# State-space mixer with expert feed-forward: scores as fp32r products over stacked halves, and zero-padded carried states

## The chip, the cores and the metric

The kernel runs on one core of one Trainium2 chip, as one launch. The metric is the device time of that launch in microseconds. The core has five engines with instruction streams of their own: PE (TensorE, matrix products), DVE (VectorE), ACT (ScalarE), POOL (GpSimd) and SP, which here only issues DMAs. They meet through semaphores.

## The reference, cut to what matters

16 sequences (called batches below) of 512 tokens with 128 channels pass through a state-space mixer, a layer norm, a routed mixture of 12 experts and a second layer norm. Everything is float32.

```python
ssm_in = x @ Win                     # gives B_ssm, C_ssm (64 each), dt_raw (8 heads), X (8 heads x 64)
delta = softplus(dt_raw + dt_bias)
# per time step and head:
h = exp(delta * neg_A) * h + X_t * (delta * B_t)
y_t = einsum('bhpn,bn->bhp', h, C_t)
y = y + D_param * X
output = (y * (silu(x @ Wz) @ Wzg)) @ Wout
x = layernorm(x + output)
# experts: hidden = gelu(sum_e dw1[:, e] * x @ W1[e].T); y = sum_e dw2[:, e] * hidden @ W2[e].T
x = layernorm(x + y + dw3 @ b2)
```

## The kernel before, in words

A batch's 512 tokens are cut into four chunks of 128. The scan becomes products: within a chunk, scores `G = B C^T` (four products of 128 x 128, `mix_scores`, L756) are weighed by decays per head and multiplied with `X` (`mix_y_within`, L920); between chunks, a state of 64 numbers per head channel is carried (`mix_states`, L802) and multiplied with the decayed `C` (`mix_y_carried`, L924). Most products are kept exact by splitting an operand into a rounded half `hi` and the rest `lo`, and running three fp32r products (`mm3`, L253 to L255); scores, both y products and the output projection are plain fp32, and each such product shows as two records in the trace.

The order of work on every engine is written out by hand in `body` (L1383). One call of it interleaves the experts of batch p with the mixer of the next batch b. Its order around the change: the last outputs of the experts of the batch before p; scores, decay rates (`mix_rates`) and chunk ends (`mix_ends`) of b; then expert 0 of p (`expert_in`, four banks of 3 products), the gate `mix_zg`, experts 1 and so on up to 11, with the heads of b between them. For each expert e, one preparation runs ahead of the products (`expert_prep`): SP fetches a row of routing weights by DMA (L1190), DVE multiplies (L1207, sends `xw`), ACT rounds (L1237, `xw_hi`), POOL takes the rest (L1241, `xw_lo`), and PE waits for `xw_lo`. For each head h, ACT scales the scores (L843), DVE adds the skip term (L852) and scans the decays (L870), POOL multiplies the two (L881, `W`). Engines take their instructions strictly in this order, so whatever stands ahead on DVE delays the next expert's multiply.

`mix_rates` also forms a running product on DVE (L710) that SP sends out and fetches back as rows (L724, L728, L747, L753); the row for expert 3 stands behind these on SP. Two PSUM banks (`mix_bank`) serve the mixer's products in turn, in the order of the table `MIX_USES`; each use waits for the reader of the one before in its bank. In the first call of `body` (b = 1) scores and rates were done ahead. Of the 16 batches, 14 (b = 2 to 15) run scores inside `body`, and 15 (b = 1 to 15) the carried products.

Of the kernel before, what the change touches and what calls it, by code (L numbers as in the profile page):

```python
# [15 lines left out]
P = 128  # L16
D = 128
NB, T = 16, 512
NC = T // P
# [23 lines left out]
    + [("X3", "Xd", 4), ("st01", "state", 2), ("st2", "state", 3)]  # L43
# [42 lines left out]
def layer_program(nc, x, Wz, Win, Wzg, Wout, dt_bias, A_log, D_param, P_w, U1T, U2T, U3T, W1T, W2T, b2, out):  # L86
    ctx = ExitStack()
    with ctx:
# [91 lines left out]
        for name, n in dict(  # L180
# [4 lines left out]
            ps_st=2, state=NC - 1, st_tmp=NC - 2, ctd=NQ, scan=H, G_dt=H, W=H,  # L185
# [8 lines left out]
        product("G_skip", H, 1, 1)  # L194
        product("xw", E, less=2)
# [62 lines left out]
        def mix_number(i, use):  # L258

            n = MIX_USE[use] % NX  # L260
            return NX - 1 - n if i == 0 and use in ("BC", "dtB") else n
# [347 lines left out]
        def mix_bc(eng, b):  # L609
# [83 lines left out]
        def mix_rates(eng, b, start=True):  # L693
# [10 lines left out]
            if eng is DVE:  # L704
# [63 lines left out]

        def mix_ends(eng, b):
# [32 lines left out]
        def mix_states(eng, b):  # L802
# [15 lines left out]
            if eng is DVE:  # L818
                for c, (use, at, k) in enumerate(place):
                    ps = bank_of(use, b)[:, at:at + N]  # L820
                    wait(DVE, "ps_st", b, k)
                    wait(DVE, "ps_ys", b.prev())
                    if c == 0:
                        sig("state", DVE.tensor_copy(S[:, 0, :], ps))
                    else:
                        wait(DVE, "state", b, c)
                        sig("st_tmp", DVE.tensor_tensor(
                            St[:, :].rearrange("p (q n) -> p q n", n=HD), S[:, c - 1, :].rearrange("p (q n) -> p q n", n=HD),
                            total[:, c * NQ:(c + 1) * NQ].unsqueeze(2).to_broadcast([P, NQ, HD]), ALU.mult))
# [1050 lines left out]
```

How the kernel before makes its waits and increments, by code:

```python
        def wait(eng, name, b, k=None):  # L219
            p = prods[name]
            v = (b.off - p.start) * p.n * p.step + ((p.n if k is None else k) - p.less) * p.step
            seen = waited.setdefault(id(eng), {})
            if (b.reg is None and v <= 0) or seen.get(name, -10**9) >= v:
                return
            seen[name] = v
            eng.wait_ge(p.sem, v if b.reg is None else b.reg * (p.n * p.step) + v)
            if eng is SP:
                alone(SP)
# [75 lines left out]
        def round_rest(n, src, hi, lo):  # L305
            DVE.tensor_copy(hi, src).then_inc(sems["chain"], 1)
            DVE.wait_ge(sems["chain"], n)
            DVE.tensor_tensor(lo, src, hi.bitcast(F32), ALU.subtract).then_inc(sems["cast"], 1)
# [1 line left out]
        def setup(eng):  # L311
# [3 lines left out]
                SP.dma_start(st_wz, Wz[:, :]).then_inc(sems["wz"], 16)  # L315
                SP.dma_start(bias_b[:, :], dt_bias.partition_broadcast(P)).then_inc(sems["decay_par"], 16)
                SP.dma_start(neg_a[:, :], A_log.partition_broadcast(P)).then_inc(sems["decay_par"], 16)
                SP.dma_start(d_b[:, :], D_param.partition_broadcast(P)).then_inc(sems["decay_par"], 16)
                SP.dma_start(st_wzg, Wzg.rearrange("(k p) n -> p k n", p=P)).then_inc(sems["wzg"], 16)
                SP.wait_ge(sems["pad"], 5)
                SP.dma_start(dA_dram.rearrange("h (c t) -> (h c) t", t=P), cum_t[0:H * NC, :]).then_inc(sems["zero"], 16)
                SP.dma_start(pw, P_w[:, :]).then_inc(sems["small"], 16)
```

## Time and profile before

| what | value |
|---|---|
| median of 3 runs | 1521.87 us (1521.78 to 1521.9) |
| the profiled execution, its own time | 1522.09 us |
| its span, first to last instruction | 1520.4 us |
| PE busy | 1504.6 us, 99% |
| DVE busy | 1128.1 us, 74% |
| POOL, ACT busy | 655.8 us, 43%; 606.0 us, 40% |
| mean granted TensorE clock | 0.999 |

"Busy" counts matrix products from start to modelled end, and these overlap, so PE at 99% says that it hardly ever stood empty. All stretches below lie in one ordinary batch between 619 and 712 us.

### The profile page before, as it was taken

To read this page: it belongs to the slowest core of one execution; us is meant where nothing else is said; L and a number is where in the kernel's file an instruction comes from. 1 tells how busy PE (TensorE), PEld (TensorE's weight loads), DVE (VectorE), ACT (ScalarE), POOL (GpSimd) and SP (SyncE) were. 2 spreads that over 40 slices of the span, in tenths; PEclk is the share of its full clock that TensorE was granted. 3 is DMA by queue.
4 is the path that set the end of the run, shared out by engine and by line. 5 is a ranking of instruction groups with operands and counts; after the bars stand their busy time and mean duration, and the time that the engine had idled before them with its cause. 6 is when DMAs were issued, how large, how long until landed. Compare 5 with 4: busy or idle time off the path is not lost.

```text
span 1520.4 us, 25377 instructions
## 1 busy us (share of the span) xinstructions
PE 1504.6 (99%) x8630; PEld 1250.7 (82%) x8630; DVE 1128.1 (74%) x3186; ACT 606.0 (40%) x1376; POOL 655.8 (43%) x747
## 2 busy tenths in 40 slices
PE   8999999999999999999999999999999999999998
PEld 7778888888888878888888888888888888888876
DVE  7797676967768677686876769777686776868755
ACT  6752424425244351533525244252443515335130
POOL 6771634616245270643606346162451715436040
PEclk9999999999999999999999999999999999999999
DMA  5350312314023040321404123140231403214020
GB/s 170 109 162 22 121 41 68 102 29 138 17 80 92 28 139 15 105 72 46 122 14 125 45 65 105 29 131 24 74 95 30 139 15 99 77 42 125 18 77 7
DMA packets 81505, 114.55 MB, mean 75 GB/s; under 512 B 10168, under 2 KB 37344, under 8 KB 81376
## 3 DMA queue, kind: packets, MB, share of 16 engines
q1 hardware_dynamic: 81376, 112.93, 24.6%
q8 instruction: 68, 1.11, 0.3%
q14 instruction: 61, 0.50, 0.1%
HBM read 107.77 MB, written 5.13 MB: 74 GB/s over the span
## 4 chain that ended last, share of the span: by engine, by line
PE 93%; POOL 2%; DVE 2%; DMA 1%; issue 1%; ACT 0%; SPq 0%; POOLq 0%; DVEq 0%; ACTq 0%
PE exp_bank L253 23%; PE exp_bank L255 22%; PE exp_bank L254 22%; PE mix_bank L964 4%; PE mix_bank L920 4%; PE mix_bank L253 3%; PE mix_bank L255 3%; PE mix_bank L254 3%; PE mix_bank L933 3%; PE mix_bank L814 1%; PE mix_bank L545 1%; PE mix_bank L762 1%; PE mix_bank L1056 1%; PE mix_bank L524 0%; POOL Wt L881 0%
## 5 line engine op out<-in xcount | busy, mean ns | idle before, releaser
L1241 POOL TENSOR_TENSOR sp_lo<-fbuf,sp_hi 128x512 fp32r<-128x512 f32 (+2 forms) x201 | 243.2, 1214 | 169.5 <-ACT sp_hi L1237 104.2
L253 PE MATMUL exp_bank<-w_hi,sp_hi 128*128 128x512 f32 x768 | 303.9, 396 | 1.2 <-POOL sp_lo L1294 0.8
L253 PE MATMUL exp_bank<-sp_hi,w_hi 128*128 128x512 f32 x764 | 302.8, 396 | 0.8 <-POOL sp_lo L1241 0.7
L255 PE MATMUL exp_bank<-w_hi,sp_lo 128*128 128x512 f32 x768 | 299.8, 390 | 0.0
L254 PE MATMUL exp_bank<-w_lo,sp_hi 128*128 128x512 f32 x768 | 299.0, 389 | 0.0
L255 PE MATMUL exp_bank<-sp_hi,w_lo 128*128 128x512 f32 x764 | 297.8, 390 | 0.0
L254 PE MATMUL exp_bank<-sp_lo,w_hi 128*128 128x512 f32 x764 | 297.5, 389 | 0.0
L1345 DVE SCALAR_TENSOR_TENSOR acc<-exp_bank,dw,acc 128x128 f32<-128x128 f32 x384 | 132.4, 345 | 163.6 <-PE exp_bank L255 162.8
L1237 ACT CAST sp_hi<-fbuf 128x512 fp32r<-128x512 f32 (+2 forms) x203 | 120.0, 592 | 270.7 <-DVE fbuf L1207 214.5
L881 POOL TENSOR_TENSOR Wt<-Wt,Gh 128x512 f32<-128x512 f32 x128 | 185.3, 1449 | 29.9 <-DVE Wt L870 29.9
L579 POOL TENSOR_TENSOR delta<-delta,bias_b 128x32 f32<-128x32 f32 x16 | 4.0, 253 | 414.3 <-ACT delta L555 409.2
L253 PEld LDWEIGHTS exp_bank<-sp_hi,w_hi 128*128 128x128 f32 x764 | 143.4, 188 | 39.3 <-issue 8.8
L870 DVE TENSOR_TENSOR_SCAN Wt<-seg_b,unit_bank 128x512 f32<-128x512 f32 x125 | 150.7, 1207 | 32.4 <-PE mix_bank L920 29.2
L255 PEld LDWEIGHTS exp_bank<-w_hi,sp_lo 128*128 128x128 f32 x768 | 144.1, 188 | 31.0
L253 PEld LDWEIGHTS exp_bank<-w_hi,sp_hi 128*128 128x128 f32 x768 | 144.3, 188 | 30.6 <-POOL sp_lo L1294 1.3
L843 ACT ACTIVATE Gh<-Gm,delta 128x128 f32<-128x128 f32 x512 | 163.7, 391 | 13.2 <-POOL Wt L881 13.2
L255 PEld LDWEIGHTS exp_bank<-sp_hi,w_lo 128*128 128x128 f32 x764 | 143.4, 188 | 30.6
L254 PEld LDWEIGHTS exp_bank<-w_lo,sp_hi 128*128 128x128 f32 x768 | 144.4, 188 | 29.0
L254 PEld LDWEIGHTS exp_bank<-sp_lo,w_hi 128*128 128x128 f32 x764 | 143.5, 188 | 28.5
L1207 DVE TENSOR_TENSOR fbuf<-turn_bank,row_b 128x512 f32<-128x512 f32 x189 | 127.1, 674 | 14.7 <-DMA row_b<-dw_rows 14.0
L1345 DVE SCALAR_TENSOR_TENSOR acc_odd<-exp_bank,dw,acc_odd 128x128 f32<-128x128 f32 x320 | 109.2, 341 | 0.0
L852 DVE SCALAR_TENSOR_TENSOR Gh<-unit_bank,d_b,Gh 128x512 f32<-128x512 f32 x120 | 88.4, 736 | 0.9 <-ACT Gh L843 0.8
(276 smaller groups left out, 2228.1 us busy)
## 6 DMA issues: line engine op xcount, KB each, us to landing
row_b<-dw_rows SPq DMA_DIRECT2D x189, 256.0 KB, 3.3
seg_b<-dA_rows SPq DMA_DIRECT2D x125, 256.0 KB, 3.4
ctd<-cum_rows SPq DMA_DIRECT2D x128, 96.0 KB, 3.2
x_in<-in_x SPq DMA_DIRECT2D x16, 256.0 KB, 2.7
result<-acc SPq DMA_DIRECT2D x15, 256.0 KB, 2.2
fbuf<-in_W1T SPq DMA_DIRECT2D x12, 256.0 KB, 4.0
acc<-in_W2T SPq DMA_DIRECT2D x4, 256.0 KB, 3.5
x_in<-in_W2T SPq DMA_DIRECT2D x4, 256.0 KB, 2.8
```

The costliest lines, as they stand in the source:

```text
L253: nc.tensor.matmul(ps, s_hi, m_hi, start=start and j == 0, stop=False, skip_group_check=onto)
L254: nc.tensor.matmul(ps, s_hi, m_lo, start=False, stop=False, skip_group_check=onto)
L255: last = nc.tensor.matmul(ps, s_lo, m_hi, start=False, stop=stop and j == n - 1, skip_group_check=onto)
L843: last = AC.activation(G[:, c, :], Gm[:, c, :], ACT.Copy, scale=delta[:, c, h:h + 1])
L852: sig("G_skip", DVE.scalar_tensor_tensor(flat, unit[:, :], d_b[:, h:h + 1], flat, ALU.mult, ALU.add))
L870: sig("scan", DVE.tensor_tensor_scan(W, first_seg[h] if first(b) else seg_b[h % 2][:, :], unit[:, :], 0.0, ALU.mult, ALU.add))
L881: sig("W", PO.tensor_tensor(W, W, Gh[h % 2][:, :, :].rearrange("p c t -> p (c t)"), ALU.mult))
L920: last = PE.matmul(ps[j * HD:(j + 1) * HD, tok(c)], Xd[:, c, h * HD:(h + 1) * HD], Wt[:, q % 2, at:at + P], start=False, stop=not opens an ...
L1207: sig("xw", DVE.tensor_tensor(wide[e % 2], rb[:, :], row_b[e % 2][:, :], ALU.mult))
L1237: sig("xw_hi", AC.copy(hi[:, cols], wide[e % 2][:, cols]))
L1241: sig("xw_lo", on.tensor_tensor(lo[:, cols], wide[e % 2][:, cols], hi[:, cols].bitcast(F32), ALU.subtract))
L1345: sig("comb", DVE.scalar_tensor_tensor(dst, ps, w, dst, ALU.mult, ALU.add))
```

## The change

Scores, from batch 2 on. ACT writes the rounded `B` to partitions 0 to 63 of a tile `BS` and DVE its rest to partitions 64 to 127; ACT and POOL write `C` rounded and rest side by side into `CS`. One fp32r product per chunk, 128 rows deep and 256 columns wide, gives two partial scores side by side, and DVE adds them with a reduction (two instructions, in place of ACT's copy `Gm`). The four products are issued in two halves: two behind rates and ends, two inside expert 0, behind its third bank. The running product moves behind both reductions on DVE. `BS` and `CS` lie in the memory of `zg`.

Carried states, from batch 1 on. Each head half has a tile of its own of 128 rows, zero in the other half's rows, so that the carried products are 128 deep, as those within a chunk are. The tiles of the first two states (`S_wide`) lie in the memory of `xT_hi` and `xT_lo`; POOL sets them to zero in each batch, ahead of expert 4's split. ACT copies the first state (two instructions), behind the scaled scores of head 0; DVE computes the other two in a new function `mix_carry`, seven instructions, which stands behind the scan of head 0, where `mix_states` stood ahead of expert 4's multiply with five.

```diff
+        S_wide = nc.alloc_sbuf_tensor_at("S_wide", [P, 2, 2, NQ * HD], F32, offset=halves_at)
...
+                if later(b):
+                    wait(AC, "ps_out", b.prev())
+                    sig("B_hi", AC.copy(BS[0:NS, :], bank_of("BC", b)[0:NS, :]))
...
+                sig("B_lo", DVE.tensor_tensor(BS[NS:2 * NS, :], bank_of("BC", b)[0:NS, :], BS[0:NS, :].bitcast(F32), ALU.subtract))
...
+                sig("C_hi", AC.copy(CS[:, 0, :], CT[:, :]))
...
+                sig("C_lo", PO.tensor_tensor(CS[:, 1, :], CT[:, :], CS[:, 0, :].bitcast(F32), ALU.subtract))
...
+        def mix_scores_half(eng, b, n):
...
+                wait(PE, "B_lo", b)
+                wait(PE, "C_lo", b)
+                ps = mix_bank(b, use)
+                for j in range(2):
+                    at = tok(2 * n + j)
+                    last = PE.matmul(ps[:, 2 * j * P:2 * (j + 1) * P].rearrange("p (k t) -> p k t", k=2), BS[:, at], CS[:, :, at],
+                                     start=True, stop=True)
+                sig("ps_G2", last)
+            if eng is DVE:
+                wait(DVE, "ps_G2", b, n + 1)
+                wait(DVE, "G_dt", b.prev())
+                sig("Gm2", DVE.tensor_reduce(Gm[:, cs, :], bank_of(use, b)[:, :].rearrange("p (c k t) -> p c t k", c=2, k=2), AX.X, ALU.add))
...
+                sig("S_zero", PO.memset(S_wide[:, :, :, :], 0.0))
+            if eng is AC and not first(b):
+                wait(AC, "ps_st", b, 1)
+                wait(AC, "S_zero", b)
+                wait(AC, "ps_ys", b.prev())
+                for j in range(2):
+                    n = slice(j * NS, (j + 1) * NS)
+                    copied = AC.copy(S_pad[0][n, j, :], bank_of("st01", b)[n, 0:N])
+                sig("state_0", copied)
...
+        def mix_carry(eng, b):
...
+                sig("st_tmp", DVE.tensor_tensor(groups(St[:, :]), groups(ps0), total_of(1), ALU.mult))
+                wait(DVE, "st_tmp", b, 1)
+                for j, n in enumerate(rows_of):
+                    last = DVE.tensor_tensor(S_pad[1][n, j, :], St[n, :], ps1[n, :], ALU.add)
+                sig("state", last)
+                wait(DVE, "state", b, 1)
+                for j, n in enumerate(rows_of):
+                    last = DVE.tensor_tensor(groups(St[n, :]), groups(S_pad[1][n, j, :]), total_of(2, n), ALU.mult)
+                sig("st_tmp", last)
+                wait(DVE, "ps_st", b, 2)
+                wait(DVE, "st_tmp", b, 2)
+                for j, n in enumerate(rows_of):
+                    last = DVE.tensor_tensor(S_pad[2][n, j, :], St[n, :], bank_of("st2", b)[n, 0:N], ALU.add)
+                sig("state", last)
...
+                    n = slice(j * NS, (j + 1) * NS) if first(b) else slice(0, P)
+                    state = (S[n, c - 1] if first(b) else S_pad[c - 1][:, j])[:, q * HD:(q + 1) * HD]
...
-                mix_scores(eng, b)
                 mix_silu_split(eng, b)
                 mix_rates(eng, b)
                 mix_ends(eng, b)
+                mix_scores_half(eng, b, 0)
+                if eng is DVE:
+                    mix_scores_half(DVE, b, 1)
+                    mix_running_product(b)
...
-                expert_in(eng, p, 0)
+                expert_in(eng, p, 0, lambda hc: hc == 2 and mix_scores_half(PE, b, 1))
...
-            mix_states(eng, b)
             if norm_before or eng is not AC:
                 mix_score_step(eng, b, 0)
+            mix_states(eng, b)
...
             mix_decay(eng, b, 0)
+            mix_carry(eng, b)
```

PE, around expert 0, before. The first three rows end the experts of the batch before; L762 are the scores, L698 to L776 rates and ends, and the next rows expert 0 (`sp_hi`, `sp_lo` are its halves).

```order
L255 MATMUL exp_bank<-w_hi,sp_lo 128x512
L762 MATMUL mix_bank<-CT,BT 128x128 x4
L698 MATMUL mix_bank<-ident,a_rows 32x128
L775 MATMUL mix_bank<-a_parts,strict_r 128x64
L776 MATMUL mix_bank<-a_parts,one_r 128x64
L253 MATMUL exp_bank<-sp_hi,w_hi 128x512
```

The same place on PE now; line numbers are those of the changed kernel (L739, L839, L840 are rates and ends, L825 the scores, L268 to L270 the three products of a split pair).

```order
L270 MATMUL exp_bank<-w_hi,sp_lo 128x512
L739 MATMUL mix_bank<-ident,a_rows 32x128
L839 MATMUL mix_bank<-a_parts,strict_r 128x64
L840 MATMUL mix_bank<-a_parts,one_r 128x64
L825 MATMUL mix_bank<-CS,BS 128x256 x2
L268 MATMUL exp_bank<-sp_hi,w_hi 128x512
```

Two of the four score products left the place between the batches, and two more (L825 again) stand inside expert 0, ahead of its fourth bank.

DVE, from the multiplies of experts 2 and 3 to that of expert 5, before:

```order
L1207 TENSOR_TENSOR fbuf<-turn_bank,row_b 128x512 x2
L824 COPY S<-mix_bank 128x256
L827 TENSOR_TENSOR St<-S,total 128x256
L831 TENSOR_TENSOR S<-St,mix_bank 128x256
L827 TENSOR_TENSOR St<-S,total 128x256
L831 TENSOR_TENSOR S<-St,mix_bank 128x256
L1207 TENSOR_TENSOR fbuf<-turn_bank,row_b 128x512
L852 SCALAR_TENSOR_TENSOR Gh<-unit_bank,d_b,Gh 128x512
L870 SCALAR_TENSOR_TENSOR Wt<-seg_b,unit_bank 128x512
L888 TENSOR_TENSOR ctd<-ctd,CT 128x384
L1207 TENSOR_TENSOR fbuf<-turn_bank,row_b 128x512
```

The same stretch of DVE now: L1318 is the experts' multiply, L958 the skip term, L976 the scan, L924 to L936 the carry, L994 the decayed C.

```order
L1318 TENSOR_TENSOR fbuf<-turn_bank,row_b 128x512 x3
L958 SCALAR_TENSOR_TENSOR Gh<-unit_bank,d_b,Gh 128x512
L976 SCALAR_TENSOR_TENSOR Wt<-seg_b,unit_bank 128x512
L924 TENSOR_TENSOR St<-mix_bank,total 128x256
L927 TENSOR_TENSOR S_wide<-St,mix_bank 64x256 x2
L931 TENSOR_TENSOR St<-S_wide,total 64x256 x2
L936 TENSOR_TENSOR S<-St,mix_bank 64x256 x2
L994 TENSOR_TENSOR ctd<-ctd,CT 128x384
L1318 TENSOR_TENSOR fbuf<-turn_bank,row_b 128x512
```

The state work moved from ahead of expert 4's multiply to between the multiplies of experts 4 and 5, and grew from five instructions to seven.

POOL, from the chunk-end products to head 0's product, now (before, there was no MEMSET, and L1241 stood there four times):

```order
L862 TENSOR_TENSOR Wt<-Xd,ends 128x512 x3
L1352 TENSOR_TENSOR sp_lo<-fbuf,sp_hi 128x512 x3
L887 MEMSET S_wide 128x1024
L1352 TENSOR_TENSOR sp_lo<-fbuf,sp_hi 128x512
L987 TENSOR_TENSOR Wt<-Wt,Gh 128x512
```

The memset came in between the splits of experts 3 and 4.

## Rows read from the trace of the kernel before

**Rows 1.** The page, part 1: busy time, share of span, instructions.

```profile
PE 1504.6 (99%) x8630; PEld 1250.7 (82%) x8630; DVE 1128.1 (74%) x3186; ACT 606.0 (40%) x1376; POOL 655.8 (43%) x747
```

**Rows 2.** Waits of PE: who for whom, us in total, times, longest.

```profile
PE exp_bank L253 <- POOL sp_lo L1241: 0.7, 1, 0.7
```

**Rows 3.** Timeline of PE: start us, us, engine, line, operation, operands, count.

```profile
619.59 1.05 PE L762 MATMUL mix_bank<-CT,BT 128*128 128x128 f32 x8
...
620.73 0.48 PE L253 MATMUL exp_bank<-sp_hi,w_hi 128*128 128x512 f32 x1
621.05 0.39 PE L254 MATMUL exp_bank<-sp_lo,w_hi 128*128 128x512 f32 x1
...
622.89 0.39 PE L253 MATMUL exp_bank<-sp_hi,w_hi 128*128 128x512 f32 x1
...
642.94 0.39 PE L253 MATMUL exp_bank<-sp_hi,w_hi 128*128 128x512 f32 x1
...
665.56 0.40 PE L1303 MATMUL turn_bank<-b_tab,bias_rows 128*128 128x256 f32 x2
665.88 1.53 PE L933 MATMUL mix_bank<-ctd,S 64*64 64x128 f32 x24
667.34 1.97 PE L920 MATMUL mix_bank<-Wt,Xd 128*64 128x128 f32 x32
```

**Rows 4.** Timeline of ACT, same batch.

```profile
619.79 0.30 ACT L1237 CAST sp_hi<-fbuf 128x128 fp32r<-128x128 f32 x1 [3.78 <-PE exp_bank L255]
...
637.47 0.62 ACT L1237 CAST sp_hi<-fbuf 128x512 fp32r<-128x512 f32 x1 [2.87 <-DVE fbuf L1207]
```

**Rows 5.** Timeline of POOL, same batch.

```profile
620.16 0.46 POOL L1241 TENSOR_TENSOR sp_lo<-fbuf,sp_hi 128x128 fp32r<-128x128 f32 x1 [2.93 <-ACT sp_hi L1237]
...
638.17 1.28 POOL L1241 TENSOR_TENSOR sp_lo<-fbuf,sp_hi 128x512 fp32r<-128x512 f32 x1 [3.05 <-DVE Gh L852]
639.42 1.61 POOL L881 TENSOR_TENSOR Wt<-Wt,Gh 128x512 f32<-128x512 f32 x1
...
661.67 1.61 POOL L881 TENSOR_TENSOR Wt<-Wt,Gh 128x512 f32<-128x512 f32 x1
```

**Rows 6.** Timeline of DVE, same batch.

```profile
622.76 0.67 DVE L710 TENSOR_TENSOR_SCAN cum_t<-dA_t,one 32x128 f32<-32x128 f32 x1
...
632.07 0.69 DVE L1207 TENSOR_TENSOR fbuf<-turn_bank,row_b 128x512 f32<-128x512 f32 x1 [0.21 <-DMA row_b<-dw_rows]
...
635.95 0.42 DVE L827 TENSOR_TENSOR St<-S,total 128x256 f32<-128x256 f32 x1
636.41 0.42 DVE L831 TENSOR_TENSOR S<-St,mix_bank 128x256 f32<-128x256 f32 x1
636.75 0.68 DVE L1207 TENSOR_TENSOR fbuf<-turn_bank,row_b 128x512 f32<-128x512 f32 x1
637.35 0.74 DVE L852 SCALAR_TENSOR_TENSOR Gh<-unit_bank,d_b,Gh 128x512 f32<-128x512 f32 x1
638.01 1.21 DVE L870 TENSOR_TENSOR_SCAN Wt<-seg_b,unit_bank 128x512 f32<-128x512 f32 x1
639.14 0.73 DVE L888 TENSOR_TENSOR ctd<-ctd,CT 128x384 f32<-128x384 f32 x1
639.79 0.68 DVE L1207 TENSOR_TENSOR fbuf<-turn_bank,row_b 128x512 f32<-128x512 f32 x1
...
661.25 0.87 DVE L888 TENSOR_TENSOR ctd<-ctd,CT 128x384 f32<-128x384 f32 x1
662.04 1.25 DVE L1006 TENSOR_TENSOR nrm<-nrm 128x4 f32<-128x4 f32 x1
```

**Rows 7.** Timeline of SP's DMA issues: four rows merged, the first for expert 3.

```profile
628.41 9.42 SPq L1190 DMA_DIRECT2D row_b<-dw_rows  x4
```

**Rows 8.** The page, part 6: DMA issues, KB each, median us to landing.

```profile
row_b<-dw_rows SPq DMA_DIRECT2D x189, 256.0 KB, 3.3
```

**Rows 9.** Groups of POOL by line and form: busy us, mean ns.

```profile
L335 POOL MEMSET BT<- 128x512 f32 x1 | 0.5, 517 | 0.0
```

More of the change, by code:

```diff
@@ L47 @@
 MIX_USE = {u[0]: n for n, u in enumerate(MIX_USES)}
+MIX_LATER = (
+    MIX_USES[:MIX_USE["G"]] + [("rates", "ends", 1), ("G01", "Gm2", 1), ("G23", "Gm2", 2)] + MIX_USES[MIX_USE["X2"]:]
+)
+MIX_LATER[MIX_USE["BC"]] = ("BC", "B_lo", 1)
+LATER_USE = {u[0]: n for n, u in enumerate(MIX_LATER)}
 MIX_FIRST = (
-    MIX_USES[:MIX_USE["X2"] + 1] + [("X3", "Xd", 4), ("st01", "state", 2), ("st2", "state", 3)]
+    MIX_USES[:MIX_USE["X2"] + 1] + [("X3", "Xd", 4), ("st01", "state", 1), ("st2", "state", 2)]
     + MIX_USES[MIX_USE["st2"] + 1:]
@@ L194, in layer_program @@
         product("G_skip", H, 1, 1)
+        for name, n in dict(ps_G2=2, Gm2=2, B_hi=1, B_lo=1, C_hi=1, C_lo=1).items():
+            product(name, n, 1, 2)
+        product("S_zero", 1, 1, 1)
         product("xw", E, less=2)
@@ L289, in first, with later @@
             return b.reg is None and b.off == 0
+        def later(b):
+            return b.off >= 2
         def bank_of(use, b):
@@ L708, in mix_rates @@
                 sig("end_sum", DVE.tensor_reduce(a_sums[:, :, :, :].rearrange("p k c h -> p k (c h)"), parts, AX.X, ALU.add))
-                wait(DVE, "rates_out", b.prev())
-                sig("ecum", DVE.tensor_tensor_scan(cum_t[R1, :], dA_t[R1, :], one[R1, :].to_broadcast([H * NC, P]),
-                                                   1.0, ALU.mult, ALU.mult))
+                if not later(b):
+                    mix_running_product(b)
             if eng is SP:
@@ L717, in mix_rates, with mix_running_product @@
                     start_rows(eng, b)
+        def mix_running_product(b):
+            wait(DVE, "dA", b)
+            wait(DVE, "rates_out", b.prev())
+            sig("ecum", DVE.tensor_tensor_scan(cum_t[R1, :], dA_t[R1, :], one[R1, :].to_broadcast([H * NC, P]),
+                                               1.0, ALU.mult, ALU.mult))
         def rates_out(b, part):
@@ L821, in mix_states @@
                     wait(DVE, "ps_st", b, k)
-                    wait(DVE, "ps_ys", b.prev())
                     if c == 0:
-                        sig("state", DVE.tensor_copy(S[:, 0, :], ps))
-                    else:
[L826 to L829, printed above, removed]
+                        sig("state_0", DVE.tensor_copy(S[:, 0, :], ps))
@@ L830, in mix_states, with groups, total_of @@
+                        wait(DVE, "state_0", b)
+                    else:
+                        wait(DVE, "state", b, c - 1)
+                        sig("st_tmp", DVE.tensor_tensor(groups(St[:, :]), groups(S[:, c - 1, :]), total_of(c), ALU.mult))
                         wait(DVE, "st_tmp", b, c)
                         sig("state", DVE.tensor_tensor(S[:, c, :], St[:, :], ps, ALU.add))
+        def groups(v):
+            return v.rearrange("p (q n) -> p q n", n=HD)
+        def total_of(c, n=slice(0, P)):
+            return total[n, c * NQ:(c + 1) * NQ].unsqueeze(2).to_broadcast([n.stop - n.start, NQ, HD])
@@ L836, in mix_score_step @@
             if eng is AC:
-                wait(AC, "Gm", b)
+                wait(AC, "Gm2" if later(b) else "Gm", b)
                 if h >= 2:
@@ L1852, in layer_program @@
         for p in prods.values():
-            written = 1 if p.name.startswith("end") and p.start else 3 if p.name != "x_in" else 2
+            written = 1 if p.name.startswith("end") and p.start else 3 if p.name not in ("x_in", "ps_G", "Gm") else 2
             count = p.done + p.less
```

65 lines of the change are left out of this document (54 added, 11 removed).

## The prediction

> **What bounds the kernel now.** I read the page first: PE is busy for 99% of the span, DVE for 74% [rows 1]. Then the waits of PE: one wait of 0.7 us for an expert's rest half is among its longest in 1520 us [rows 2], so in an ordinary batch PE runs without a gap, and its own instructions are the time. Two things can move it: fewer or cheaper products, and a new wait. For the second I read one batch on all engines in order of time, and asked at each place that the change touches how much later PE's supplier may come.
>
> **Scores, on PE.** Four fp32 products take from 619.59 to about 620.48, when the rates begin: 0.89 us, 0.11 per record [rows 3]. The new ones are 256 columns of fp32r. The only such row is L1303: two in 0.40 us with the drain of the last (0.28), so 0.12 apart; up to the next group at 665.88 it is 0.16 each, with a change of tile shape in it [rows 3]. I take 0.11 to 0.12. Four cost 0.46 in place of 0.89: 0.43 us a batch, 6.0 us over 14 batches, if nothing else held PE.
>
> Something does. Expert 0 needs the rest of its last token chunk. Its source is read by PE's last product of the batch before, so ACT starts only behind that, at 619.79 for 0.30 [rows 4], and POOL follows at 620.16 for 0.46, to 620.62 [rows 5]. PE starts expert 0 at 620.73 [rows 3], about 0.1 us after POOL is done. So the 1.14 us of scores, rates and ends ahead of it just cover this chain, which the change leaves alone. With two score products of 0.23 in place of 0.89, PE has 0.48 us to do there and then waits some 0.66. Expert 0 still starts at 620.7, and the other two products now stand inside it as pure addition: 0.23, and 0.09 because a wide product behind short ones is followed late (620.73 to 621.05 is 0.32, where wide ones come 0.23 apart) [rows 3]. Scores therefore cost PE +0.31 a batch and gain nothing.
>
> **Carried products, on PE.** They keep their count, 24 records, and their columns. Solve two groups for pace and opening: L933 runs 1.53 us with 0.27 drain over 11 steps of two records, L920 1.97 over 15 [rows 3]; so a step is 0.11 in both, and the opening of each costs 0.05. Depth 64 or 128 makes no difference to the pace. Between the groups, L933's last step starts at 667.14 and L920 at 667.34: 0.09 more than a step. With one shape in both, opening and gap go: 0.14, twice a batch, 0.28 us, times 15 batches: -4.2 us. The bounds are 0 (the gap belongs to the wait for W) and 0.4 a batch.
>
> The Trainium skill, TensorEngine Tiling (Array Packing), Key Properties, says that a change of tiling mode drains the engine, and its table of speedups credits small contraction depth with up to 2x. By the first, the gain above is right; by the second, padding to 128 rows could double these products. The trace speaks for the first alone, since L920 at depth 128 keeps L933's pace; the second is the last rival below.
>
> **DVE, ACT, POOL, SP: first, how late the state becomes.** The other score product of expert 0 starts at 622.89 + 0.11 = 623.00 and ends 0.28 later. A reduction that reads 512 numbers per partition costs about what the multiply L1207 does, 0.69 [rows 6] (bounds 0.5 and 1.2). It starts at 623.3, and the running product behind it at 623.93, where it started at 622.76 [rows 6]: 1.17 late. SP's rows, and behind them the row of expert 3, first issued at 628.41 [rows 7], move with it. DVE waited for that row already at 632.07 [rows 6], so expert 3's multiply comes at 633.24. From there multiply, cast and split take 0.69 + 0.04 + 0.62 + 0.08 + 1.28, with durations and handovers from 636.75 to 638.17 [rows 4 to 6]: POOL is done at 635.95. In itself that hurts nobody, as PE needs expert 3 near 637.5. But the memset now follows: 512 columns took 0.52 [rows 9], so 1024 at most 1.03, less a fixed part: 0.95, to 636.9. ACT's two state copies wait for it. I price them at 0.42 each, as DVE's of 256 columns, overlapping a little: 637.65. ACT's cast of expert 4 is queued behind them, and ends at 638.3; POOL's split is at 638.35 to 639.63. PE wants expert 4 at about 640.5: hidden, by 0.9.
>
> **Then the carry.** DVE no longer works on states ahead of expert 4's multiply, so this comes as soon as its row is there: SP may issue it behind expert 2's multiply, near 632.2, and a row lands in 3.3 [rows 8]: 635.5, where it was 636.75 [rows 6]. Behind it 0.60, 0.66 and 1.13 (the starts from 636.75 to 639.14) bring the carry's first instruction to 637.9 [rows 6]. A dependent step costs 0.46 to 0.52 (635.95 to 636.41), an independent one 0.34 (636.41 to 636.75) [rows 6]. Halves of 64 rows have the same columns, so I price them like whole ones. The first product of a stored state (L931) then starts at 637.9 + 0.46 + 0.34 + 0.52 = 639.2.
>
> L931 reads two operands from SBUF, and there POOL and DVE get in each other's way. L888, of that kind, started at 639.14 and took 0.73 for 384 columns, ending 0.41 after POOL's split ended (638.17 + 1.28) [rows 5, 6]. More to the point: at 661.25 L888 ran, POOL's product started at 661.67, and the tiny L1006, queued behind L888, took 1.25 us for 4 columns, until POOL ended [rows 5, 6]. So between two such DVE instructions a waiting POOL instruction goes first, and takes its full 1.3. The Trainium skill, SBUF — State Buffer, Who interferes with whom, has the rule: a DVE instruction with two SBUF inputs contends with a GpSimd one that reads SBUF, and issue order decides who blocks. The trace agrees with both halves of it. For the carry: the first L931 waits for expert 4's split until 639.63, and ends at 639.9; POOL's product of head 0, ready, takes 1.27 to 641.2; the second L931 ends at 641.5; two adds and the decayed C bring 0.05 + 0.34 + 0.34 + 0.45. Expert 5's multiply starts at 642.6, where it was 639.79 [rows 6]. If DVE keeps the port for both, 641.7; if POOL is out of the way altogether, 641.4.
>
> From the multiply to PE it takes 0.68 + 0.04 + 0.62 + 0.08 + 1.28 + 0.08 = 2.8, and the first product after a wait costs 0.11. PE starts expert 5 at 645.5; it started at 642.94 [rows 3]: 2.56 us late. This swallows the 0.31 of the scores. Against it stand the 0.28 of the tile shapes: +2.28 a batch; with the port kept +1.4, with POOL out of the way +1.1. The starting point of each step is the late one of its bounds, and a row or a memset that comes 0.5 sooner passes part of that on, so I take 2.0. What is late next: from expert 5 to expert 8 DVE's cycle with one head, 2.4 to 3.0 (636.75 to 639.79 is 3.04), is about PE's 2.7 per expert (12 products 0.23 apart); the y products of heads 0 to 3 follow expert 6, and such a pair of groups (1.46 and 1.9 us [rows 3]) gives over 3 us of air. So one stall a batch.
>
> **The sum.** 14 batches x 2.0 = 28. Batch 1 has no new scores; it trades its own state work on DVE for two instructions more, +0.5, and gains 0.28: +0.2. The other additions are hidden: ACT's cast of C (0.6) and POOL's rest of C (1.3) stand in front of over 2.5 us in which each waits for PE's last output [rows 4, 5]; DVE's rest of B lies in its own idle time. They cost up to 0.6 a batch if the rest of C came later than the rates. 1522.09 + 28.2 = 1550.3 for the profiled execution, whose time lies 0.2 above the median of the runs: 1550.
>
> **Rivals.**
> 1. The state work is hidden or nearly so: rows land sooner, the copies are shorter, DVE and POOL don't collide. For it: DVE is idle for a quarter. Against: seven instructions in one piece stand between two multiplies 3.04 apart, and PE's slack at expert 5 is 0.4 (639.79 + 2.8 against 642.94). With a stall of up to 1 us, 1522 + 14 x (0 to 1) = 1522 to 1536; at the lower end the scores' +0.31 and the shapes' -0.28 cancel, and it is 1522, no change.
> 2. Faster: PE is not held by POOL at expert 0, and the stall does not come. The place is expert 0's start, the price 0.43 + 0.28 a batch: 1522.1 - 6.0 - 4.2 = 1512. It decides if the cast and split of 128 columns start 0.66 sooner; nothing in the diff moves them, and both bounds must fail at once.
> 3. Padding costs the array's sharing: if the two halves no longer ran side by side, a record would take the scores' 0.11 in place of 0.055: 48 x 0.055 = 2.6 us a batch, 40 us more: 1590. Against it, L920's pace.
>
> **Chances.** Forecast, with its own range 1540 to 1557: 0.60. Rival 1: 0.22, of which 0.06 is no change. Rival 2: 0.07. Rival 3: 0.03. Above 1557 by a longer collision: 0.08. The range 1529 to 1557 leaves out the faster cases, the lowest part of rival 1 and what lies above. A measurement tells 0.2%, 3 us, from no change: faster 0.07, same 0.06, slower 0.87.
>
> **What would show it.** PE's score products in two groups of two, and a wait for POOL's rest half of about 0.6 us in front of expert 0, 14 times; L920's counterpart following the carried group by 0.11; ACT waiting for the memset; one of the two L931 counterparts about 1.2 us long; a wait of PE for POOL's split at expert 5, 1.2 to 2.4 us. If expert 5's multiply comes under 3.4 us behind expert 4's, or PE shows no wait there, I am wrong.

## The result, and the profile after

The changed kernel takes 1578.4 us in the median of 6 runs (1570.1 to 1581.5), against 1521.8 of before (1521.3 to 1522.0): a ratio of 1.0366, 95% interval 1.0343 to 1.0389, or 56.6 us more. I had forecast 1550, with 1557 as the upper end: slower, but by half as much as it is. The profiled execution took 1581.5 with a span of 1579.8, and 59.4 us more than the profiled one of before is what has to be found.

The page after, part 1, and below it PE's largest wait (who for whom: us in total, times, longest):

```profile
PE 1520.2 (96%) x8574; PEld 1249.3 (79%) x8574; DVE 1205.3 (76%) x3258; ACT 615.5 (39%) x1406; POOL 687.1 (43%) x777
```

```profile
PE exp_bank L268 <- POOL sp_lo L1352: 42.8, 32, 2.9
```

PE was busy for 99% [rows 1] and waited for such a rest 0.7 us in all [rows 2]; now it waits 42.8 us, 32 times, about twice a batch: briefly at expert 0, and for long at expert 5. The timeline of PE in an ordinary batch of after, which stands beside [rows 3]; its last product of the batch before starts at 741.41, where that one's started at 619.36:

```profile
741.88 0.48 PE L825 MATMUL mix_bank<-CS,BS 128*128 128x256 f32 x2
742.72 0.50 PE L268 MATMUL exp_bank<-sp_hi,w_hi 128*128 128x512 f32 x1 [0.35 <-POOL sp_lo L1352]
...
744.64 0.39 PE L270 MATMUL exp_bank<-sp_hi,w_lo 128*128 128x512 f32 x1
745.13 0.50 PE L825 MATMUL mix_bank<-CS,BS 128*128 128x256 f32 x2
745.47 0.40 PE L268 MATMUL exp_bank<-sp_hi,w_hi 128*128 128x512 f32 x1
...
755.97 1.51 PE L878 MATMUL mix_bank<-Wt,B_tok 128*64 128x256 f32 x12
...
765.50 0.39 PE L270 MATMUL exp_bank<-sp_hi,w_lo 128*128 128x512 f32 x1
768.01 0.50 PE L268 MATMUL exp_bank<-sp_hi,w_hi 128*128 128x512 f32 x1 [2.12 <-POOL sp_lo L1352]
...
773.68 0.66 PE L1043 MATMUL mix_bank<-ctd,S_wide 128*64 128x128 f32 x8
...
775.04 1.92 PE L1026 MATMUL mix_bank<-Wt,Xd 128*64 128x128 f32 x32
```

Start to start, from the last product of the batch before: expert 0 at 1.31 (before 1.37), the states at 14.56 (before 13.82), expert 5 at 26.60 (before 23.58). The carried groups and what follows them start 1.36 apart (773.68 to 775.04), where it was 1.46 [rows 3], and what stands behind both starts 3.20 behind the first, where it was 3.36 (665.88 to 669.24). A batch of before lasts 92.43 us, this one 95.29; such ordinary batches lie between 95.3 and 95.6.

The states are the row of L878, and the first row of each expert is found by its place. Summed over the span:

| part of the 59.4 us | forecast | measured |
|---|---|---|
| batches 2 to 15, each as an ordinary one | 14 x 2.0 = 28.0 | 14 x 2.87 = 40.2 |
| batch 1 (104.3 before, 111.4 after) | 0.2 | 7.1 |
| PE at its lower clock in batches 2 to 15: 38 wide products 0.43 apart in place of 0.23 | 0 | 7.8 |
| longer waits in some of them | 0 | 4.3, the rest |

The longest of these waits, 2.9 us, come in the batches that start at 451.6 and 547.8. There DVE waits 1.8 and 2.2 us for expert 3's row, and 0.7 to 1.3 in the others. That row lands late in a batch of before too, which lasts 93.07.

The work on the states in the same batch, by engine (DVE, ACT, POOL), beside [rows 4 to 6]; between the second and the third row of DVE stand the skip and the scan, and the first row is expert 2's multiply:

```profile
753.97 0.68 DVE L1318 TENSOR_TENSOR fbuf<-turn_bank,row_b 128x512 f32<-128x512 f32 x1
...
757.97 0.69 DVE L1318 TENSOR_TENSOR fbuf<-turn_bank,row_b 128x512 f32<-128x512 f32 x1 [1.69 <-DMA row_b<-dw_rows]
...
760.37 0.40 DVE L924 TENSOR_TENSOR St<-mix_bank,total 128x256 f32<-128x256 f32 x1
760.80 0.85 DVE L927 TENSOR_TENSOR S_wide<-St,mix_bank 64x256 f32<-64x256 f32 x2
761.68 2.08 DVE L931 TENSOR_TENSOR St<-S_wide,total 64x256 f32<-64x256 f32 x2
763.80 0.85 DVE L936 TENSOR_TENSOR S<-St,mix_bank 64x256 f32<-64x256 f32 x2
...
765.27 0.69 DVE L1318 TENSOR_TENSOR fbuf<-turn_bank,row_b 128x512 f32<-128x512 f32 x1
```

```profile
759.28 0.75 ACT L894 COPY S_wide<-mix_bank 64x256 f32<-64x256 f32 x2 [1.17 <-POOL S_wide L887]
760.05 0.62 ACT L1348 CAST sp_hi<-fbuf 128x512 fp32r<-128x512 f32 x1
```

```profile
758.23 0.96 POOL L887 MEMSET S_wide<- 128x1024 f32 x1
760.75 1.30 POOL L1352 TENSOR_TENSOR sp_lo<-fbuf,sp_hi 128x512 fp32r<-128x512 f32 x1 [1.56 <-ACT sp_hi L1348]
762.00 1.48 POOL L987 TENSOR_TENSOR Wt<-Wt,Gh 128x512 f32<-128x512 f32 x1
```

Expert 5's multiply comes 7.30 us behind expert 4's (757.97 to 765.27); it was 3.04 [rows 6]. The seven instructions of the carry take 4.3 of it, and the two L931 take 2.08 where the pairs of adds beside them, of the same size, take 0.85.

### The profile page after: what moved, and what is told of

Read it like the earlier page. It is cut to its first block, busy times and chain, and to the rows that moved or that the text cites. A ratio compares the mean times of both kernels' runs of the same rounds, so it can differ in the third digit from the quotient of the medians.

```text
span 1579.8 us, 25429 instructions
## 1 busy us (share of the span) xinstructions
PE 1520.2 (96%) x8574; PEld 1249.3 (79%) x8574; DVE 1205.3 (76%) x3258; ACT 615.5 (39%) x1406; POOL 687.1 (43%) x777
## 4 chain that ended last, share of the span: by engine, by line
PE 74%; DVE 11%; DMA 5%; issue 4%; POOL 4%; ACT 1%; SPq 1%; POOLq 0%; DVEq 0%; ACTq 0%
PE exp_bank L268 18%; PE exp_bank L269 18%; PE exp_bank L270 18%; PE mix_bank L1074 4%; DMA row_b<-dw_rows 3%; PE mix_bank L1026 3%; PE mix_bank L1043 3%; PE mix_bank L268 3%; PE mix_bank L270 2%; PE mix_bank L269 2%; DVE St L931 2%; DVE fbuf L1318 2%; POOL sp_lo L1352 2%; DVE Gh L958 1%; DVE acc L1460 1%
## 5 line engine op out<-in xcount | busy, mean ns | idle before, releaser
L268 PE MATMUL exp_bank<-sp_hi,w_hi 128*128 128x512 f32 x764 | 309.8, 405 | 42.9 <-POOL sp_lo L1352 42.8
L268 PE MATMUL exp_bank<-w_hi,sp_hi 128*128 128x512 f32 x768 | 303.5, 395 | 1.2 <-POOL sp_lo L1406 0.8
L269 PE MATMUL exp_bank<-sp_lo,w_hi 128*128 128x512 f32 x764 | 302.0, 395 | 0.0
L270 PE MATMUL exp_bank<-sp_hi,w_lo 128*128 128x512 f32 x764 | 301.6, 395 | 0.0
L270 PE MATMUL exp_bank<-w_hi,sp_lo 128*128 128x512 f32 x768 | 299.5, 390 | 0.0
L268 PEld LDWEIGHTS exp_bank<-sp_hi,w_hi 128*128 128x128 f32 x764 | 145.7, 191 | 91.2 <-POOL sp_lo L1352 53.9
L976 DVE TENSOR_TENSOR_SCAN Wt<-seg_b,unit_bank 128x512 f32<-128x512 f32 x125 | 150.9, 1209 | 37.1 <-PE mix_bank L1026 34.3
L270 PEld LDWEIGHTS exp_bank<-sp_hi,w_lo 128*128 128x128 f32 x764 | 145.8, 191 | 32.1
L268 PEld LDWEIGHTS exp_bank<-w_hi,sp_hi 128*128 128x128 f32 x768 | 144.3, 188 | 30.7 <-POOL sp_lo L1406 1.3
L270 PEld LDWEIGHTS exp_bank<-w_hi,sp_lo 128*128 128x128 f32 x768 | 144.1, 188 | 30.4
L1318 DVE TENSOR_TENSOR fbuf<-turn_bank,row_b 128x512 f32<-128x512 f32 x189 | 127.5, 677 | 47.4 <-DMA row_b<-dw_rows 46.8
L958 DVE SCALAR_TENSOR_TENSOR Gh<-unit_bank,d_b,Gh 128x512 f32<-128x512 f32 x120 | 88.7, 739 | 1.5 <-ACT Gh L949 1.4
```

What stands on the lines that cost most here:

```text
L268: nc.tensor.matmul(ps, s_hi, m_hi, start=start and j == 0, stop=False, skip_group_check=onto)
L269: nc.tensor.matmul(ps, s_hi, m_lo, start=False, stop=False, skip_group_check=onto)
L270: last = nc.tensor.matmul(ps, s_lo, m_hi, start=False, stop=stop and j == n - 1, skip_group_check=onto)
L958: sig("G_skip", DVE.scalar_tensor_tensor(flat, unit[:, :], d_b[:, h:h + 1], flat, ALU.mult, ALU.add))
L976: sig("scan", DVE.tensor_tensor_scan(W, first_seg[h] if first(b) else seg_b[h % 2][:, :], unit[:, :], 0.0, ALU.mult, ALU.add))
L1318: sig("xw", DVE.tensor_tensor(wide[e % 2], rb[:, :], row_b[e % 2][:, :], ALU.mult))
```

## The experiments

Medians in us; each ratio is against runs of the kernel before on the same chip. "Stretches" are starts of PE's groups, subtracted.

**e1: the carried states alone.** The change without its scores: `mix_scores`, B, C and the running product as before.

> Only the carried states are changed (padded tiles, copies on ACT, memset on POOL, carry in seven DVE instructions behind expert 4's multiply); the scores stay four fp32 products. My theory after the result: an ordinary batch of the changed kernel is 2.9 us longer, 2.3 of it the stall of PE at expert 5, and batch 1 is 7.1 us longer by two stalls (experts 4 and 5). Both belong to this half. Without the new scores the rows come about 1.2 us sooner and PE reaches expert 5 0.75 us sooner, so the stall stays near 2 us: 1522 + 14 x (2.0 - 0.3) + 7 = 1553, between 1546 and 1562, with batch 1 (its y0 stretch 13.9 us before) at 20 to 22 us. Rival: the carry is late only because the scores made the rows late; then the stall is under 1 us a batch and the time 1522 + 7 + 14 x (0 to 0.7), 1529 to 1539.

1567.8, ratio 1.0306 (1.0290 to 1.0322). Both theories missed: above mine, far above the rival. PE reaches the states on time (13.82), its products at expert 5 are 2.1 to 2.6 us apart all the same (twice 3.2 to 3.3), and ordinary batches last 94.1 to 94.6. So the stall is the states' own. The new scores put expert 2's multiply, and expert 4's row behind it, about 0.75 later in the batch (12.56 in place of 11.81, and 15.6 to 16.0 in e1 become 16.4 to 17.1), and PE comes as much later: the stall moves with them and keeps its length. Batch 1 takes 110.3, so its loss belongs here too. What I had left out was the clock: 7 later batches (the expectation counted 8) have 7 or 8 wide products each 0.43 apart. PE's timeline of one:

```profile
756.07 0.39 PE L260 MATMUL exp_bank<-sp_hi,w_lo 128*128 128x512 f32 x1
758.43 0.50 PE L258 MATMUL exp_bank<-sp_hi,w_hi 128*128 128x512 f32 x1 [1.98 <-POOL sp_lo L1294]
...
759.44 0.63 PE L258 MATMUL exp_bank<-sp_hi,w_hi 128*128 128x512 f32 x1
759.87 0.63 PE L259 MATMUL exp_bank<-sp_lo,w_hi 128*128 128x512 f32 x1
```

**e2: the scores alone.** The change without its states.

> Only the scores are changed (stacked halves, one fp32r product per chunk from batch 2 on, running product behind two reductions); the carried states are as before. My theory: expert 0 starts where it did (1.37 us behind the last product of the batch before, held by POOL's rest), the second pair of products adds 0.6 us (0.26 of it a wait for the bank that ACT's total still reads), and the rows, 1.2 us later, still land inside the wait for the states: +0.76 a batch, 1522 + 14 x 0.76 = 1532.5, between 1529 and 1537, batch 1 unchanged. Rival A: the late rows also stall an expert, +1.5 a batch or more: over 1540. Rival B: the narrower products pay and the time falls to 1512 to 1518.

1534.2, ratio 1.0081 (1.0065 to 1.0096): as expected. Expert 0 at 1.31, the states at 14.56, no stall at expert 5, batches of 93.2 to 93.8, clock 0.999. The two halves add up: 45.8 + 12.3 = 58.1 against 56.6.

**e3: is PE held at expert 0?** From batch 2 on the kernel leaves out three of the four score products.

```
+        def norm_later(b):
+            return b.off >= 2
...
-                for c in range(NC):
+                for c in range(1 if norm_later(b) else NC):
                     last = PE.matmul(ps[:, tok(c)], BT[:, tok(c)], CT[:, tok(c)], start=True, stop=True)
```

> The kernel before, with one of the four score products left out three times over (from batch 2 on only chunk 0's scores are computed). It asks whether PE is held at expert 0. Theory: the chain from PE's last product through ACT's cast and POOL's rest of 128 columns sets expert 0's start at 1.31 to 1.37 us behind that product, so 0.67 us less of PE's work a batch buys at most 0.06: 1521 to 1522. Rival: the time follows PE's work, 14 x 0.67 = 9.4 us less: 1512.5.

1521.3, ratio 0.9997 (0.9988 to 1.0007). 0.67 us of products a batch are gone, expert 0 starts 0.06 sooner, and a batch lasts 92.35 in place of 92.43. PE is held there: of the scores' 0.9 us nothing can be gained while the cast and the rest of 128 columns stand behind PE's last product.

**e7: the second pair of score products later** (edit on e2).

```
-                expert_in(eng, p, 0, lambda hc: hc == 2 and mix_scores_half(PE, b, 1))
+                expert_in(eng, p, 0, lambda hc: hc == 3 and mix_scores_half(PE, b, 1))
```

> e2 (scores alone changed) with the second pair of products one step later inside expert 0, behind its twelfth product instead of its ninth. Theory: in e2 the pair's first product starts 0.49 us behind the wide one ahead of it, 0.26 more than a wide one takes, because it waits for the bank that ACT's total still reads; 0.68 us later the bank is free, so the stretch up to the states shrinks by 0.2 to 0.3 a batch: 1534.2 - 14 x 0.26 = 1530.6. Rival: the 0.26 is what such a pair costs behind wide products wherever it stands: 1534.

1534.7, ratio 1.0087 (1.0071 to 1.0104): no gain. The time is the rival's, but its reason isn't: the pair got cheaper, as the theory had it, and the time came back elsewhere. Timeline of PE, and the weight load that stands first behind it:

```profile
814.54 0.40 PE L818 MATMUL mix_bank<-CS,BS 128*128 128x256 f32 x2
814.77 0.40 PE L263 MATMUL mix_bank<-wx_hi,xT_hi 128*128 128x512 f32 x1
...
815.24 0.39 PE L265 MATMUL mix_bank<-wx_hi,xT_lo 128*128 128x512 f32 x1
815.72 0.49 PE L263 MATMUL mix_bank<-sp_hi,wzg_hi 128*128 128x512 f32 x1
```

```profile
815.72 0.19 PEld L263 LDWEIGHTS mix_bank<-sp_hi,wzg_hi 128*128 128x128 f32 x1 [0.52 <-DVE Gm L824]
```

The pair now costs 0.23 in all (814.54 to 814.77), where in the changed kernel 744.64 to 745.47 is 0.83, 0.60 more than one wide product: the bank is free, and a product of 256 columns costs 0.11 to 0.12, as I had priced it. But the next user of the pair's bank waits for DVE's reduction instead (815.24 to 815.72), and another for a copy behind it. With two banks in turn, one more use with a slower reader costs the same in both places tried.

**e6: the zeros of batch 1 earlier** (edit on the changed kernel).

```
             if not norm_before:
                 split_w(eng, [N1 + 3])
+                if eng is PO:
+                    zero_pads(b)      # the two memsets of mix_states
```

> The changed kernel, with one edit in batch 1 alone: POOL's two memsets stand in front of the split of expert 3 and of a weight, in a gap of POOL, instead of behind them. Theory: in batch 1 the memset ends at 83.4, ACT's state copies and its cast of expert 4 wait for it, and DVE's carry for the copies (2.34 us idle); moved, the first of the two stalls (1.7 us) goes and the second shrinks by 1 to 2 us with part of the low clock behind it: batch 1 is 3 to 6 us shorter, 1578 becomes 1572 to 1575. Rival: batch 1's loss is the seven instructions like any other batch's and the memset hides nothing: within 1 us of the changed kernel, the y0 stretch of batch 1 still 21 us.

1573.4 (1567.5 to 1576.3), ratio 1.0325 (1.0299 to 1.0352). Batch 1 falls from 111.4 to 106.8 with one stall in place of two. The chain that went, in the changed kernel (POOL, behind a weight's split and a smaller memset; ACT; DVE):

```profile
81.99 0.53 POOL L886 MEMSET S<- 128x512 f32 x1
82.46 0.95 POOL L887 MEMSET S_wide<- 128x1024 f32 x1
```

```profile
83.49 0.75 ACT L894 COPY S_wide<-mix_bank 64x256 f32<-64x256 f32 x2 [3.54 <-issue]
84.26 0.62 ACT L1348 CAST sp_hi<-fbuf 128x512 fp32r<-128x512 f32 x1
```

```profile
84.27 0.43 DVE L924 TENSOR_TENSOR St<-mix_bank,total 128x256 f32<-128x256 f32 x1 [2.34 <-ACT S_wide L894]
```

The page's "issue" for ACT is the wait for the zeros: the copy starts 0.08 behind the memset's end (83.41).

**e8: POOL's product out of the carry's way** (edit on e1: for POOL alone `mix_decay(b, 0)` stands behind expert 5's split).

```
-            mix_decay(eng, b, 0)
+            if eng is not PO or not norm_before:
+                mix_decay(eng, b, 0)
...
                 experts(eng, p, [e], ahead)
+                if q == 0 and eng is PO and norm_before:
+                    mix_decay(eng, b, 0)
```

> e1 (states alone changed) with POOL's product of head 0 put behind its split of expert 5, so that POOL has nothing to do between its split of expert 4 and that of expert 5, while DVE does the carry. Theory: of the two multiplies of a stored state (2.08 us for both, where the adds of the same size take 0.85) the second loses 1.25 to that product; without it expert 5's multiply comes 1.25 sooner and the stall falls from 2.1 to 2.4 to about 1.0: 1567.8 - 14 x 1.25 = 1550, less up to 8 more if the granted clock comes back to 1.00: 1542 to 1552. Rival: the port is no cause, or the late product makes ACT and DVE late for head 2 as much: 1560 or more.

1566.5, ratio 1.0294 (1.0277 to 1.0311): the theory's 1542 to 1552 missed, as the rival had it. Timelines of DVE, of ACT, and of POOL:

```profile
657.66 0.93 DVE L874 TENSOR_TENSOR St<-S_wide,total 64x256 f32<-64x256 f32 x2
...
665.38 0.75 DVE L901 SCALAR_TENSOR_TENSOR Gh<-unit_bank,d_b,Gh 128x512 f32<-128x512 f32 x1 [2.23 <-ACT Gh L892]
```

```profile
664.06 1.28 ACT L892 ACTIVATE Gh<-Gm,delta 128x128 f32<-128x128 f32 x4 [2.62 <-POOL Wt L930]
```

```profile
662.75 2.53 POOL L930 TENSOR_TENSOR Wt<-Wt,Gh 128x512 f32<-128x512 f32 x2
```

The two multiplies take 0.93 in place of 2.08, and the products at expert 5 are 1.1 to 1.4 us apart (2.0 to 2.3 in three batches of 14). That is the theory's half. The rival's half holds too: the product comes late for ACT's scores of head 2, expert 6's cast is queued behind them, and there products are 1.7 to 1.8 us apart. An ordinary batch is 0.7 longer than in e1 (95.0 against 94.3), the lower clock is gone but for batch 1 and one other (0.997), and the two cancel.

**e9: PE's wait filled** (edit on e1).

```
+                if e == 4 and b.off >= 1 and not last_batch(b):
+                    for _ in range(8):
+                        last = PE.matmul(hb[NH - 1][:, :], w1_hi[:, e, w], lo, start=False, stop=False)
```

> e1 (states alone changed) with 8 more wide products a batch, which repeat expert 4's last one (so the expert sums are not the reference's), put in front of PE's wait at expert 5. They fill 1.8 of its 2.1 to 2.6 us. Theory: the low clock (products 0.43 us apart in place of 0.23 behind such a wait, in 8 of e1's 14 later batches, worth 1.7 us each) follows a PE that stands still; with the wait filled the clock stays up, and a kernel with 112 more products is faster: 1567.8 - 8 x 1.7 = 1554, between 1552 and 1559, granted clock 0.996 or more (batch 1 isn't filled). Rival: the low clock has another cause (what DVE, POOL and the DMAs do then); the time stays at 1566 to 1570 with the clock at 0.991 to 0.994.

1557.5, ratio 1.0235 (1.0218 to 1.0252), clock 0.998: 10.3 us faster than e1 with 112 products more. PE, the same place:

```profile
754.25 1.97 PE L1317 MATMUL exp_bank<-sp_lo,w_hi 128*128 128x512 f32 x8
...
756.16 0.50 PE L258 MATMUL exp_bank<-sp_hi,w_hi 128*128 128x512 f32 x1
756.50 0.40 PE L259 MATMUL exp_bank<-sp_lo,w_hi 128*128 128x512 f32 x1
```

The eight take the place of the wait. Outside batch 1, which isn't filled, no product lies 0.43 apart. The rest of the kernel keeps its pace (an ordinary batch lasts 94.2 to 94.5, as e1's do where the clock stays up), so the low clock came from PE's standing still.

**e4: DVE in four whole instructions, ACT pads** (edit on e1, core of it; the memset stands as in the change, but from batch 2 on).

```
+            if eng is DVE and b.off >= 2:
...
+                sig("st_tmp", DVE.tensor_tensor(groups(St[:, :]), groups(ps0), total_of(1), ALU.mult))
...
+                sig("state", DVE.tensor_tensor(S[:, 0, :], St[:, :], ps1, ALU.add))
...
+                sig("st_tmp", DVE.tensor_tensor(groups(St[:, :]), groups(S[:, 0, :]), total_of(2), ALU.mult))
...
+                sig("state", DVE.tensor_tensor(St[:, :], St[:, :], bank_of("st2", b)[:, 0:N], ALU.add))
...
+        def pad(b, c, src):
+            for j in range(2):
+                n = slice(j * NS, (j + 1) * NS)
+                last = AC.copy(S_pad[c][n, j, :], src[n, :])
```

DVE's four stand in `mix_states`, ahead of expert 4's multiply. ACT's copies stand ahead of expert 4's cast and behind score steps 1 and 3.

> Scores as before; from batch 2 on the padded product shape as in the change, but DVE carries the states in four whole instructions where the kernel before did it (ahead of expert 4's multiply, the first reading PSUM directly), and ACT writes all six half copies into the padded tiles in its own gaps; batch 1 stays unpadded. Theory: the two changes of tile shape per pair of groups are worth 0.30 us a batch, as the changed kernel's rows show (3.36 to 3.21, twice), and nothing waits for the copies: 1522 - 14 x 0.30 = 1517.7, 1516 to 1519. Rival: the memset on POOL and the copies on ACT push a split or a cast past the 0.4 us of slack at expert 5, and the gain is lost: 1521 to 1530, with a wait of PE for POOL's split.

1518.6 (11 runs, 1517.3 to 1519.4) against 1522.0: ratio 0.9976 (0.9967 to 0.9985), as expected, and faster than both kernels, though by only 0.2% against before. Timeline of DVE, then of PE at the first pair of y groups:

```profile
633.50 0.42 DVE L842 TENSOR_TENSOR St<-mix_bank,total 128x256 f32<-128x256 f32 x1 [1.01 <-PE mix_bank L822]
...
634.94 0.42 DVE L849 TENSOR_TENSOR St<-St,mix_bank 128x256 f32<-128x256 f32 x1
635.27 0.68 DVE L1261 TENSOR_TENSOR fbuf<-turn_bank,row_b 128x512 f32<-128x512 f32 x1
```

```profile
664.96 0.66 PE L987 MATMUL mix_bank<-ctd,S_wide 128*64 128x128 f32 x8
...
666.32 1.92 PE L968 MATMUL mix_bank<-Wt,Xd 128*64 128x128 f32 x32
```

A batch lasts 92.11, 0.32 under before. Batch 1 is unpadded in e4, e5 and e10, so they also save what it loses in the change and in e1 (7.1 and 6.0 us).

**e5: the same four, late** (edit on e4: the four stand behind expert 4's multiply, skip and scan, where the change has its seven, and ACT copies the first two states together, behind score step 2).

> Scores as before. Padded states from batch 2 on with ACT writing all copies, and DVE's carry in four whole instructions, as in e4, but put where the change has it: behind expert 4's multiply, skip and scan. It asks whether the place or the number of instructions makes the stall. Theory: seven instructions take 4.3 us there (760.37 to 764.68 in the changed kernel's trace), four take 1.8, or 2.6 if one waits for POOL; expert 5's multiply comes 1.7 to 2.5 sooner than in e1, whose stall was 2.1 to 2.4, so 0 to 0.6 us stays: 1517.7 + 14 x (0 to 0.6) = 1518 to 1526, with the granted clock at 1.00. Rival: the place alone does it (ACT's cast of expert 4 behind copies, the row late); then over 1.5 us stays: 1539 or more.

1535.8, ratio 1.0092 (1.0075 to 1.0109), between the two expectations. The stall at expert 5 is gone: four instructions take 2.2 us, one of them 0.97 beside POOL. A wait of 0.9 (products 1.1 apart) stands at expert 6, and ACT's timeline shows why:

```profile
647.24 0.73 ACT L872 COPY S_wide<-mix_bank 64x256 f32<-64x256 f32 x2
648.00 0.82 ACT L872 COPY S_wide<-S 64x256 f32<-64x256 f32 x2
648.85 0.62 ACT L1295 CAST sp_hi<-fbuf 128x512 fp32r<-128x512 f32 x1
```

Expert 6's multiply was done at 647.87; four copies stood ahead of its cast. That is my placing of them, not the carry's.

**e10: both halves, with e4's carry.**

> Both halves of the change, with e4's way of carrying the states (four whole DVE instructions ahead of expert 4's multiply, copies on ACT, from batch 2 on). Theory: the halves add up, so this costs what the scores alone cost, less the tile shapes: 1518.6 + (1534.2 - 1522.0) = 1530.8, between 1529 and 1534, with no wait at expert 5 over 0.5 us. Rival: the late rows of the scores and the copies on ACT together exceed the slack at expert 5 and a stall of 1 us or more comes back: over 1540.

1529.5, ratio 1.0054 (1.0038 to 1.0071). Batches of 92.86, no wait at expert 5. With the stall gone, the changed scores are what makes the kernel slower.

## Why the prediction was half right

It was right in the direction and in the place of the stall. The forecast for the profiled execution was 31.2 us short: 12.2 in the ordinary batches, 6.9 in batch 1, 7.8 at the lower clock and 4.3 in longer waits. I had given 0.08 to a time above 1557, by a longer collision of DVE and POOL; the collision was as forecast, and the time went above for other reasons.

- **Expert 0 held by POOL: right.** It starts at 1.31 as against 1.37, with a wait of 0.35 in its row (I said 0.66, which counted the drain of the products as free time), and e3 shows the hold.
- **"The other two products stand inside it as pure addition: 0.23, and 0.09": wrong in size.** They cost 0.60 a batch, and 0.17 follows within the zg products. The products are as cheap as I said (e7); I had not followed the bank. The second pair takes the bank of the rates, which ACT's exponentials leave at 745.08, 0.05 before the pair starts. e7 shows that another wait takes its place.
- **The tile shapes: right**, about 0.3 for the 0.28 forecast (twice 3.36 to 3.20, and 0.32 in e4). TensorEngine Tiling (Array Packing) of the Trainium skill, Key Properties, has the drain at a change of mode, and this agrees; its table under Theoretical Speedup, on which my third rival drew, does not show here: a carried group of 24 records and the step behind it take 1.36 at depth 128 and 1.46 at depth 64.
- **The carry and the stall at expert 5: right in place and cause, a little small.** Forecast 7.1 from multiply to multiply and a start 2.56 late; measured 7.30 and 3.02. Expert 4's row landed 0.4 later than I had it, the carry took 0.2 more. The two L931 took 0.65 and 1.42 (in all 15 batches the second takes 1.42): the second lost 1.0 to POOL's product, and in e8 it takes 0.42, both 0.93. This is what SBUF — State Buffer of the Trainium skill, Who interferes with whom, says of a DVE instruction with two SBUF inputs and a GpSimd one, here 2.08 us in place of 0.93.
- **"So I take 2.0": wrong.** My own sum gave 2.28; I took it down because late steps pass on part of their delay. Nothing was passed on: 2.87. Nor was it right that the stall "swallows the 0.31 of the scores": what the scores cost PE ahead of it (0.75 from batch start to the states, by the bank) also delays expert 2's multiply and expert 4's row, which accounts for the 0.4 above, and the stall starts later at its full length. Alone, the states cost 1.7 to 2.2 a batch (e1, where the clock stays up) and the scores 0.8 or a little more (e2); together 2.87. This is 12.2 of the 31.2 us.
- **Batch 1, "+0.5 ... +0.2": wrong, 7.1.** I counted its instructions and not its queues. There POOL also splits weights, has a second memset, and ACT's copies and its cast of expert 4 stand behind both (e6: 4.7 us). What I had asked of a moved step for batches 2 to 15 I did not ask for the one batch with another order.
- **No term for the clock: 7.8 us, and 2.6 within batch 1's 7.1.** In the changed kernel, PE's rows behind its longest wait, and the stretches around it (us, PE, PEld, DVE, ACT and POOL busy, granted clock, DMA share, GB/s):

```profile
575.66 0.50 PE L268 MATMUL exp_bank<-sp_hi,w_hi 128*128 128x512 f32 x1 [2.90 <-POOL sp_lo L1352]
...
576.61 0.63 PE L268 MATMUL exp_bank<-sp_hi,w_hi 128*128 128x512 f32 x1
577.04 0.63 PE L269 MATMUL exp_bank<-sp_lo,w_hi 128*128 128x512 f32 x1
```

```profile
574.00:576.00 2.00, 0.34 (x2) 0.30 (x3) 2.00 (x4) 1.43 (x5) 1.67 (x2) 1.00 0.44 98
576.00:578.00 2.00, 2.00 (x7) 1.58 (x6) 2.00 (x3) 1.74 (x5) 2.00 (x2) 0.56 0.54 189
```

  PE falls from 2.4 to 1.2 GHz after the wait, for 6 to 12 wide products. It does so in 5 of the 14 batches, with waits that the others have too: after 1.9 us of standing still in one batch it falls, after 2.9 us in another it doesn't. The runs' spread of 11 us goes with it: the fastest (1570.1) has a mean clock of 0.999, the slowest (1581.5) 0.991, the four between them 0.993 or 0.994. Before shows no such product; from 25 us on it has no wait of PE over 0.9 us. What decides between batches with the same wait stays open.

Of my three tests, "expert 5's multiply under 3.4 us behind expert 4's, or no wait there" did not come: they are 7.30 and 2.12. "One stall a batch" held in ordinary batches. "ACT waiting for the memset" is the row of 759.28, harmless there.

## What to carry to other kernels

A stall of the engine that bounds the kernel is priced twice: once as its length, once as the slower products behind it; a nearly full TensorE that begins to wait 2 us a batch lost 10 to 12 us in 1580 to the clock alone, and filling the wait with useless products won 10 us back. Work that moves onto a busy engine is best kept in few whole instructions, with the halves, copies and padding on an engine that has gaps (in the change's own place, four in place of seven bring an ordinary batch from 94.1 to 94.6 in e1 down to 93.2 to 93.5 in e5, with no low clock; ahead of expert 4's multiply, in e4, it is 92.11). And a step is followed through every batch that has an order of its own, and a product through the bank that it writes, before either is called free.

## What the runs showed of the hardware

- More products, less time: e9's 112 added wide products, 25 us of PE's time at 0.227 each, made the kernel 10.3 us faster, as they stood in waits.
- An engine with less to do let POOL start earlier, and so blocked DVE. ACT no longer copies the scores, so POOL's rest of silu starts at 742.73, just ahead of DVE's add of `acc` at 742.99, which took 1.17 us where it took 0.29. It does so in all 14 batches, and in e2, but not in e1. Behind it stand the sums that free the rates' bank.
- Two copies of 64x256 from PSUM on ACT took 0.75, and a memset of 1024 columns on POOL 0.96, near what I had (0.75 and 0.95).
